# Gate and up projections as seven block products instead of eight, weights split once for both batches

## The reference

```
h = x
g = einsum('bsd,edf->ebsf', h, Wg)          # 8 experts, F = 1024
u = einsum('bsd,edf->ebsf', h, Wu)
expert_outs = einsum('ebsf,efd->ebsd', silu(g) * u, Wd)
expert_output = einsum('be,ebsd->bsd', gating_probs, expert_outs)
shared = (silu(h @ Sg) * (h @ Su)) @ Sd      # one expert more, with weight sg
x = x + (1 - sg) * expert_output + sg * shared
...
attn_in = tanh(x @ W1 + b1);  scores = attn_in @ v
p = softmax(masked scores)                   # before / after / all but the own token, by prompt type
x = x + (p @ x) / cnt
```

## Time and profile before

| | us |
|---|---|
| median of 3 runs | 1240.72 (1239.9 to 1240.99) |
| span of the profiled execution | 1241.5 |
| TensorE matmul busy | 1232.6 (99%) |
| VectorE busy | 734.6 (59%) |
| GpSimd busy | 602.0 (48%) |
| ScalarE busy | 199.2 (16%) |

### The profile page before, as it was taken

One profiled execution on the slowest core, in us unless ns is written; L12 is line 12 of the kernel. 1 busy time (PEld: TensorE's weight loads), 2 busy tenths in 40 slices (PEclk: granted clock), 3 DMA queues, 4 the chain that ended last, 5 costly groups with the idle time before them and its releaser, 6 DMA issues.

```text
span 1241.5 us, 15497 instructions
## 1 busy us (share of the span) xinstructions
PE 1232.6 (99%) x5409; PEld 1007.1 (81%) x5409; DVE 734.6 (59%) x963; ACT 199.2 (16%) x342; POOL 602.0 (48%) x640
## 2 busy tenths in 40 slices
PE   8999999999999999999999999999999999999998
PEld 7888888888888888888888888888888888887765
DVE  5655655656556565565655656556555565555756
ACT  2111111111111111111111111111111111111222
POOL 6855549596444444444444444444444444443301
PEclk9999999999999999999999999999999999999997
DMA  5111111112111111111111111111111111101001
GB/s 170 54 51 49 38 40 51 51 34 68 51 51 51 51 40 36 50 51 51 51 51 51 51 51 42 35 50 51 51 51 51 51 51 51 48 33 47 1 9 59
DMA packets 63981, 61.07 MB, mean 49 GB/s; under 512 B 4576, under 2 KB 63968, under 8 KB 63968
## 3 DMA queue, kind: packets, MB, share of 16 engines
q1 hardware_dynamic: 63680, 60.90, 15.7%
q10 hardware_dynamic: 288, 0.01, 0.0%
HBM read 58.80 MB, written 2.10 MB: 49 GB/s over the span
## 4 chain that ended last, share of the span: by engine, by line
PE 99%; DVE 0%; DMA 0%; ACT 0%; SPq 0%; issue 0%
PE gate_ps L720 11%; PE acc L720 11%; PE gate_ps L721 11%; PE gate_ps L724 11%; PE acc L724 11%; PE acc L721 11%; PE up_ps L720 10%; PE up_ps L724 10%; PE up_ps L721 10%; PE spare L778 1%; PE acc L820 0%; DMA x_nat<-in_x 0%; PE spare L801 0%; PE acc L825 0%; PE acc L809 0%; PE gate_ps L809 0%
## 5 line engine op out<-in xcount | busy, mean ns | idle before, releaser
L541 DVE SCALAR_TENSOR_TENSOR h<-gate_silu,gates,up_ps 128x512 f32<-128x512 f32 x288 | 215.3, 748 | 455.6 <-PE up_ps L724 455.6
L317 POOL TENSOR_TENSOR wd_hi<-raw_d,zero 128x256 fp32r<-128x256 f32 x144 | 92.1, 639 | 541.0 <-PE acc L724 541.0
L548 DVE TENSOR_TENSOR h_lo<-h,h_hi 128x512 fp32r<-128x512 f32 x288 | 326.1, 1132 | 9.9
L420 ACT ACTIVATE gate_silu<-gate_ps 128x512 f32<-128x512 f32 x288 | 172.4, 599 | 985.0 <-PE gate_ps L724 985.0
L720 PE MATMUL gate_ps<-xT_hi,wgu_hi 128*128 128x512 f32 x576 | 225.0, 391 | 1.3 <-DVE xT_lo L530 1.3
L721 PE MATMUL gate_ps<-xT_hi,wgu_lo 128*128 128x512 f32 x576 | 224.2, 389 | 0.0
L720 PE MATMUL acc<-h_hi,wd_hi 128*128 128x512 f32 x576 | 224.2, 389 | 0.0
L720 PE MATMUL up_ps<-xT_hi,wgu_hi 128*128 128x512 f32 x576 | 224.2, 389 | 0.0
L724 PE MATMUL gate_ps<-xT_lo,wgu_hi 128*128 128x512 f32 x576 | 224.1, 389 | 0.0
L724 PE MATMUL up_ps<-xT_lo,wgu_hi 128*128 128x512 f32 x576 | 224.1, 389 | 0.0
L721 PE MATMUL acc<-h_hi,wd_lo 128*128 128x512 f32 x576 | 224.1, 389 | 0.0
(11 more groups left out here) (118 smaller groups left out, 663.3 us busy)
## 6 DMA issues: line engine op xcount, KB each, us to landing
raw_gu<-in_L_cond_Wg SPq DMA_DIRECT2D x64, 256.0 KB, 2.7
raw_gu<-in_L_cond_Wu SPq DMA_DIRECT2D x64, 256.0 KB, 3.3
raw_d<-in_L_cond_Wd SPq DMA_DIRECT2D x64, 256.0 KB, 3.6
x_nat<-in_x SPq DMA_DIRECT2D x8, 256.0 KB, 6.9
raw_gu<-in_L_cond_Sg SPq DMA_DIRECT2D x8, 256.0 KB, 2.7
raw_gu<-in_L_cond_Su SPq DMA_DIRECT2D x8, 256.0 KB, 3.2
raw_d<-in_L_cond_Sd SPq DMA_DIRECT2D x8, 256.0 KB, 3.7
out_x<-x_nat SPq DMA_DIRECT2D x8, 256.0 KB, 2.1
```

What stands on the lines that cost most here:

```text
L317: nc.gpsimd.tensor_tensor(wd_hi[:, f, :], raw_d[:, s, j, :], zero[:, 0:1].broadcast_to([P, D]), ALU.add).then_inc(d_hi_done, 1)
L420: nc.scalar.activation(gate_silu[:, u % 2, :], gate_ps[:], ACT.Silu).then_inc(silu_done, 1)
L541: nc.vector.scalar_tensor_tensor(out=h[:, i, :], in0=gate_silu[:, i, :], scalar=gate_of[:, bass.ds(step, 1)], in1=up_ps[:], op0=ALU.mult, ...
L548: nc.vector.tensor_tensor(h_lo[:, s, :], h[:, i, :], h_hi[:, s, :].bitcast(F32), ALU.subtract).then_inc(h_split, 1)
```

## The change

Gate and up of one hidden tile are now made for both halves of the tokens in one piece, a group: 2 batches x 9 experts x 8 tiles = 144 groups. With two blocks k, two halves t, and the pair gate and up, a group is a 2x2 by 2x2 product of blocks. Before that was eight block products; now it is seven (a Strassen scheme), each in three passes.

- The seven products need sums of blocks of x and of the weights. `combine_x` (VectorE) makes the four sums of x once per batch, and all seven blocks are split into `xs_hi` and `xs_lo`. `combine` (GpSimd) makes the four sums of the weights of a pair of tiles, and `split_tile` splits seven blocks of a tile at a time (128x896).
- Products go into three kinds of banks, `g_ps`, `e_ps` and `v_ps`. Product 1 is needed in two results, so ScalarE copies it from `g_ps` into `v_ps` (`seed`), PSUM to PSUM, before product 2 is added to `g_ps` and products 6, 5 and 3 to `v_ps`. ScalarE also copies product 7 (`keep_p7`) and the sum of products 1 and 6 (`keep_v`) into SBUF. VectorE adds them: `second_gate` and `second_up`.
- ScalarE rounds h to its high part (`round_h`), which VectorE did. VectorE still makes h (`hidden_second`, now with two inputs in SBUF, and `hidden_first`) and its low part (`rest_h`).
- Experts are walked in chunks of four tiles: four groups of batch 0, then four of batch 1 with the same split weights (`RING` = 6 tiles). The shared expert goes through once per batch. So 80 tiles are loaded and split, and not 144. After each chunk VectorE adds `acc` to `xT` (`add_acc`).
- No queue loops: all are written out. The second layer of batch 0 lies between groups 137 to 143.

The core of it on TensorE, ScalarE and VectorE:

```diff
-            def unit(b, u, step):
-                gate(b, u, step)
-                down((u - LAG) % UNITS, step if u >= LAG else step - 1)
-                up(b, u, step)
...
+            for i in range(NG):
+                if i == L1_AT:
+                    pe.wait_ge(const_step, CONST_STEPS)
+                p4(i)
+                p5(i)
+                if i + 1 < NG:
+                    gate_start(i + 1)
+                if i:
+                    down(0, i - 1)
+                first_bank(i - L1_AT)
+                if i + 1 < NG:
+                    gate_end(i + 1)
+                p3(i)
+                if i + 1 < NG:
+                    p7(i + 1)
+                    p6(i + 1)
+                if i:
+                    down(1, i - 1)
+                second_bank(i - L1_AT)
...
+            def gate_end(i):
+                pe.wait_ge(seeded, i + 1)
+                product(2, i, g_ps, False)
...
+            def seed(i):
+                act.wait_ge(p_done[1], i + 1)
+                if i >= 2:
+                    act.wait_ge(h_done[0], i - 1)
+                nc.scalar.activation(v_ps[i % 2][:], g_ps[:], ACT.Copy).then_inc(seeded, 1)
...
+            for i in range(NG):
+                gate_second(i)
+                if i + 1 < NG:
+                    seed(i + 1)
+                round_h(1, i)
+                first_bank(i - L1_AT)
+                if i + 1 < NG:
+                    gate_first(i + 1)
+                    keep_p7(i + 1)
+                    keep_v(i + 1)
...
+                round_h(0, i)
+                second_bank(i - L1_AT)
...
+            for i in range(NG):
+                second_gate(i)
+                second_up(i)
+                second_layer(i - L1_AT)
+                hidden_second(i)
+                if i >= 2 and groups[i - 2][3]:
+                    add_acc(1, i - 2)
+                rest_h(1, i)
+                if i >= 1 and groups[i - 1][3]:
+                    add_acc(0, i - 1)
...
+                hidden_first(i)
+                rest_h(0, i)
```

And the weights on GpSimd:

```diff
+            def combine(s, cols):
+                w = raw[:, s, :, cols]
+                n = cols.stop - cols.start
+                t_made(nc.gpsimd.tensor_tensor(w[:, 4:6, :], w[:, 1:4:2, :],
+                                               w[:, 0:1, :].broadcast_to([P, 2, n]), ALU.subtract))
+                t_made(nc.gpsimd.tensor_tensor(w[:, 6, :], w[:, 3, :], w[:, 4, :], ALU.add))
+                t_made(nc.gpsimd.tensor_tensor(w[:, 7, :], w[:, 2, :], w[:, 6, :], ALU.subtract))
...
+                    if n >= RING:
+                        pool.wait_ge(p_done[3], final_group[n - RING] + 1)
...
+                    split(w[:, 1:8, :], hi, lo, NP, gu_hi_done, n + 1, gu_split)
+                split_d(n)
```

More of the change, by code:

```diff
@@ L19 @@
 from contextlib import ExitStack
+from math import prod
 import concourse.bass as bass
@@ new lines, in rest_h, with add_acc @@
+            def rest_h(t, i):
+                dve.wait_ge(h_hi_done[t], i + 1)
+                nc.vector.tensor_tensor(h_lo[t][:, i % 2, :], h[t][:], h_hi[t][:, i % 2, :].bitcast(F32),
+                                        ALU.subtract).then_inc(h_split[t], 1)
+            def add_acc(t, i):
+                b = groups[i][0]
+                half = slice(t * BANK, (t + 1) * BANK)
+                dve.wait_ge(down_done[t], i + 1)
+                for d in range(KD):
+                    nc.vector.tensor_tensor(xT[:, b, d, half], acc[d][t][:], xT[:, b, d, half],
+                                            ALU.add).then_inc(acc_read[t], 1)
@@ new lines, in p6, with p4, p5, p3 @@
+            def p6(i):
+                product(6, i, v_ps[i % 2], False)
+            def p4(i):
+                pe.wait_ge(p7_copied, i + 1)
+                product(4, i, e_ps, False)
+            def p5(i):
+                pe.wait_ge(v_copied, i + 1)
+                product(5, i, v_ps[i % 2], False)
+            def p3(i):
+                pe.wait_ge(up1_done, i + 1)
+                product(3, i, v_ps[i % 2], False)
+            def down(t, i):
+                b, n, first, end = groups[i]
+                if i == first_group[n]:
+                    pe.wait_ge(d_split, n + 1)
+                if first and acc_before[i]:
+                    pe.wait_ge(acc_read[t], KD * acc_before[i])
+                elif first:
+                    pe.wait_ge(xT_copied, B * KD * NT)
+                pe.wait_ge(h_split[t], i + 1)
@@ L782, in score_row @@
-            def score_row(b):
-                for t in range(NT):
-                    pe.wait_ge(tanh_done, b * NT + t + 1)
-                    nc.tensor.matmul(SCORE[b][t][:], v_rep[:], attnT[:, b, t * BANK:(t + 1) * BANK],
-                                     start=True, stop=True).then_inc(score_done, 1)
+                    mm = three_pass(acc[d][t][:], wd_hi[:, n % RING, cols], wd_lo[:, n % RING, cols],
+                                    h_hi[t][:, i % 2, :], h_lo[t][:, i % 2, :], first, end)
```

888 lines of the change are left out of this document (503 added, 385 removed).

## The result

| | before | after |
|---|---|---|
| median | 1240.86 us (4 runs) | 1255.84 us (1255.44 to 1257.21, 4 runs) |
| ratio | | 1.0113 (95% interval 1.0096 to 1.013) |
| profiled execution: span | 1241.5 us | 1254.4 us |

The change makes the kernel 1.1% slower, a small difference, but its interval is clear of 1. The prediction said 1190, 1155 to 1230. Slower was its rival C, with a chance of 0.07, but not by rival C's mechanism.

What follows compares the result with a forecast made beforehand. The prediction took TensorE, busy 99% of the span, as the bound: number of matmuls by the time of one. 1241.5 - 97.9 + 30 + 11.5 + 4 + 2 = 1191.1 us profiled; forecast 1190 us, range 1155 to 1230.

Steps and rivals of the forecast that it cites:

- rival C: At product 2, low part of h0 locks in on GpSimd's 2.28 us pass, 90 times: 1265 us, slower; chance 0.07.
- Term 1: On TensorE, 33 matmuls per group instead of 36, 432 fewer at 0.2267 us each: -97.9 us.
- a group lasts 7.48 us if TensorE never waits: TensorE's steady group: its length without waits, from which the slack of 0.87 us at product 2 was worked out.
- Matmuls 0.2267 apart: Sign on TensorE that would show the forecast right: matmuls start 0.2267 us apart.
- Term 2: Steady part: VectorE's instructions with two SBUF inputs wait out GpSimd's passes in some 90 groups: +30 us, bounds 0 and 67.
- a random arrival waits beyond 0.87, on average: VectorE meeting a full GpSimd: average wait beyond the slack 0.21 us, plus 0.12 passed on by two earlier instructions.
- fall into gaps ahead of `hidden_first`: VectorE's 136 chunk-end adds at 0.68 us were taken to fit its gaps, so undisturbed TensorE is never late.
- drift: GpSimd's tile takes 8.6 us and the group 7.48, so collisions would not lock in; the argument against rival C.
- Term 3: Start: GpSimd's supply of tiles decides, fourth group near 46 us: +11.5 us, bounds 4 and 20.
- Terms 4 and 5: Second layer: scans and joins delay `hidden_second`, +4 us; end: block sums wait for e_diag, +2 us.
- A (no collisions): Steady part: GpSimd's passes fall beside VectorE's, so no such waits: 1160 us; chance 0.24.
- D: TensorE's written-out instruction stream or the clock costs; 1% for fetching is 12 us, giving 1202 us; chance 0.04.

Runs made afterwards that it cites:

- e5: Kernel before, with 64 unused bytes ahead of the split weights, so weights and h start 64 bytes further on: 1272.66 us, ratio 1.0255.
- e7: Changed kernel with split weights, x's blocks and h moved back to the offsets of the kernel before: 1243.72 us, ratio to before 1.0015.
- e10: Kernel before, with only the split weights 64 bytes further on: 1276.1 us.
- e17: Kernel before, with only the split weights 512 bytes further on: 1247.1 us.
- e3: Changed kernel with GpSimd's weight passes cut to one element from the seventh tile on (output not correct): 1207.22 us, ratio to before 0.9738.
- e8: Changed kernel with each 896-element GpSimd pass in two pieces, four blocks and three: 1209.66 us, ratio to before 0.9738.
- e4: Changed kernel with h and its low part ahead of batch 1's sums, these spread over groups 0 to 3: 1255.15 us, ratio to before 1.0116.
- e12: As e9, with batch 1's sums and low parts in order of need and GpSimd leaving tiles 4 and 5 until they are done: 1181.68 us.
- e13: Kernel before, with x's split, the split weights and h all 64 bytes further on: 1240.1 us.
- e2: Kernel before, with TensorE's loop over steps written out and nothing else changed: 1241.93 us, ratio 0.9989.
- e11: Kernel before, with only the split x and h 64 bytes further on and the weights left: 1253.2 us.
- e9: Changed kernel with the edits of both e7 and e8: 1190.44 us, ratio to before 0.9585.

## Why the prediction was wrong, step by step

The prediction's sum was 1191.1 us in the profiled execution; it was 1254.4. The forecast came out too low by 63 us. To set the terms apart, the two traces are cut at the same counts of first-layer matmuls, 512 columns each. The first 171, up to group 6, take 83.2 us after and 55.1 before. The last 291, with all that follows, take 130.6 and 116.0. Between them lie groups 6 to 135, 4290 matmuls in 1040.6 us; at the 0.22667 of before they would take 972.4, and before there were 432 more. The pace is 4752 x 0.00533 = 25.3 us over all three stretches, and is taken out of the other rows.

| term | predicted | measured | shown by |
|---|---|---|---|
| 1, fewer matmuls | -97.9 | -97.9, and +25.3 for the pace | e5, e7, e10 to e17 |
| 2, waits in the steady part | +30 | +45.3 | e3, e8 |
| 3, start | +11.5 | +27.2 | e4 and e12, in part |
| 4 and 5, second layer and end | +6 | +13.0 | trace; 3 of them go with e8 |

**Term 1, the count right, the price wrong.** 432 matmuls went. The step that failed is "432 x 0.2267", taken on with "a group lasts 7.48 us if TensorE never waits": it lasted 7.64 to 7.67. "Matmuls 0.2267 apart" was among the text's own signs, and it is the one that failed. I took the 0.2267 of the rows for a property of the matmul; it is a property of the matmul and of where its operands lie, and the change moved them all. No view of the profile before shows this, but the allocation in the diff does: the old kernel placed tensors of round sizes one behind the other; the new one counts bytes by hand, with a region of 8224 bytes (8 x 257 x 4) per batch in it, which puts what comes behind 32 bytes further off the grid each time. The Trainium skill, "TensorE: Matmul & The Clock Gate", section "Wait — 56ns, not 53.3ns?", gives 215.7 ns; no run here came below 226.7. The Trainium skill, "SBUF — State Buffer", section "Who interferes with whom", lists the read ports for moving operand and weight load as independent. `e10` against `e13`, 233.3 against 226.7 ns by nothing but relative place, shows that in this kernel the two do not run independently of where their operands lie.

**Term 2, the mechanism right, place and size off.** VectorE does wait for a whole pass of GpSimd when both its inputs lie in SBUF, and h with an input in PSUM does not (L717 averages 739 ns, L709 1118). That was the prediction's mechanism, and the rule of the locked pair of ports that the Trainium skill, "SBUF — State Buffer", section "Who interferes with whom", states holds in every row shown. What failed is "a random arrival waits beyond 0.87, on average" 0.21. It treated the three instructions as independent and let only what they passed on count 0.12. In the trace they hit three passes in a row, since GpSimd is full and its passes follow without a gap: in the group shown `hidden_second` and the low part behind it are 2.58 us late together (2.18 and 1.84 instead of 0.75 and 0.69), where the text allowed 1.67. The chunk's adds, which were to "fall into gaps ahead of `hidden_first`", stand behind them in the same queue, 1.27 us more. Nor are the arrivals random, nor do 90 groups wait a little each: the pattern repeats once per chunk of four tiles, the waits for `h_lo` fall on the same two of eight groups, and GpSimd and the groups do not "drift" against each other over many groups, as the text said against rival C. A reason that fits is that GpSimd waits for TensorE once per chunk (16 waits, 367.6 us in all). And TensorE waits first at the down product for `h_split`: from 84 to 1080 us 28.7 of the 43.3 us that starts come late, and 14.6 at `seeded`; I had worked out slack for `seeded` alone. The text named this place as one that would refute it, and did not compute it. That cutting a pass in two removes every wait, not half of them, fits this: when delays add up in a queue against a fixed slack, shorter ones can stay below it altogether. The runs show the effect; that this is its whole reason is my reading.

**Term 3, the wrong engine.** "GpSimd decides instead" gave 46 us for the fourth group; it began at 51.4, nine us after GpSimd had its gate and up blocks ready. TensorE waited 6.39 us for VectorE's `h_lo` instead. `e4`, which takes VectorE's queue out of the way at that point, gives 44.8, near the predicted number, but by luck: there too the blocks were ready three us before. The term left out batch 1's four sums and seven low parts on VectorE, and the slow matmuls behind each wait. The bound of 20 was too low as well.

**Terms 4 and 5.** The block sums waited 5.29 us for `e_diag`, and ran in 5.97 where they had taken 3.63: 7.6 us against the 2 predicted. First the changed kernel, then the kernel before:

```profile
1208.73 5.97 PE L1001 MATMUL v_ps<-x,e_diag 128*8 128x257 f32 x16 [5.29 <-DVE e_diag L808]
```

```profile
1197.86 3.63 PE L809 MATMUL gate_ps<-x,e_diag 128*8 128x257 f32 x16
```

No experiment was made on this. Of the rest of the 13 us, some 3 go with `e8`; what remains was not taken apart.

**The rivals.** A (no collisions) is what `e8` and `e3` come near to in the steady part. C's place was wrong: product 2 is not where most of the time goes, though its idea of a collision that locks in and repeats was closer to the trace than the random arrival of the forecast. D's written-out program costs nothing on TensorE in the kernel before (`e2`); D's clock did fall, but at the start, where it averages 0.88 over 84 us. None had the pace. Without it the changed kernel takes 1243.7 us (`e7`), no better than before: waits, start and end use up what the fewer matmuls bring.

**What was right:** ScalarE's copy into PSUM took 0.58 us (0.60 taken), the share of DMA fell from 15.7% to 8.8%, `hidden_first` and the adds with a PSUM input stayed constant. GpSimd's busy time, put near 550, was 607.1 us: the time in which its passes wait for VectorE's counts in it (`wd_hi` averages 0.82 us, undisturbed 0.61).

## What to carry to other kernels

When a change moves tensors in SBUF, compare TensorE's start-to-start time where nothing waits before explaining anything else; keep weights and moving operands at the same remainder of 256 bytes, which was worth 31 us in the kernel before (`e5`), and 12 to 19 us in the changed one. Where VectorE and GpSimd both work from SBUF, it is the length of GpSimd's single instruction against VectorE's slack that costs, not the sum of their work: two pieces instead of one pass were worth 46 us, with more instructions in all. And when two engines are both released by a third, look for a schedule that repeats before averaging over arrivals. Work out the slack of every wait on the main engine's path, and add up all delays of one queue within one round before comparing them with it.

## What the runs showed of the hardware that was not expected

- Matmuls of 128x512 in fp32r, each with its own weight load, start 226.7 ns apart if weights and moving operands agree modulo 256 bytes in their start, and up to 233.3 ns on average if not (`e10`), with the same instructions. The slow pace is a fixed pattern: in `e10` the intervals alternate between 230.9 and 235.9 ns, in `e11` they go round 225.9, 229.1 and 231.7.
- After a wait of 5.29 us, sixteen small matmuls took 5.97 us instead of 3.63. From 1203 to 1215 us, where they lie, the granted clock averages 0.72, a mix of 2.4 and 1.2 GHz:

```profile
1203.00:1215.00 12.00, 6.71 (x20) 2.21 (x20) 3.39 (x9) 6.38 (x14) 0.00 (x0) 0.72 0.00 0
```

- A faster engine can uncover waits: restoring the pace was worth 12 us with the long passes (`e7`) and 19 us with the short ones (`e8` to `e9`).
